# Attention step with scores and keys in alternation, maxima in the middle, batch work last but one

## What is computed

```python
qkv = jnp.einsum('bsh,oh->bso', hidden_states, w_qkv)      # hidden_states: normalized rows
scores = jnp.einsum('bhqd,bhkd->bhqk', q, k) * scale
scores = jnp.where(causal, scores, jnp.finfo(scores.dtype).min)
probs = jax.nn.softmax(scores, axis=-1)
attn = jnp.einsum('bhqk,bhkd->bhqd', probs, v)
return jnp.einsum('bsh,oh->bso', attn, w_o)

x = x + 0.5 * _L0_ffn_ref(_layernorm(x, axis=-1), ...)
x = x + _L0_attn_ref(_layernorm(x, axis=-1), L0_attn_w_qkv, L0_attn_w_o)
x = x + 0.5 * _L0_ffn_ref(_layernorm(x, axis=-1), ...)
```

## Time and profile before

| | us |
|---|---|
| median of 3 runs (857.02 to 858.62) | 858.06 |
| profiled execution, its own time | 857.71 |
| span of the profiled execution | 856.0 |
| mean granted TensorE clock, share of full | 0.966 |

### The profile page before, as it was taken

How to read it: one execution, slowest core, us unless ns; L and a number is a source line. 1 busy time by engine, 2 the same in 40 slices (tenths; PEclk the granted TensorE clock), 3 DMA queues, 4 the chain that set the end, 5 groups by cost and what they waited for, 6 DMA issues and landing times. The chain is left out here.

```text
span 856.0 us, 15881 instructions
## 1 busy us (share of the span) xinstructions
PE 766.5 (90%) x6126; PEld 669.7 (78%) x6126; DVE 445.2 (52%) x848; ACT 370.0 (43%) x611; POOL 310.7 (36%) x363
## 2 busy tenths in 40 slices
PE   5789999999999988878788887866799999999997
PEld 3469999999999975555555554444699999999997
DVE  7755444634553037566666576256554446345530
ACT  4215445534553111555554556423154455345531
POOL 3164454455413361141321122201644544554133
PEclk9999999999999996989999999898999999999999
DMA  9434554254322242221022010052345543543222
GB/s 331 115 98 114 140 139 114 60 150 128 93 55 26 26 160 88 77 77 73 7 77 101 21 59 28 20 179 53 95 111 144 139 111 65 150 127 92 58 25 25
DMA packets 60070, 80.27 MB, mean 94 GB/s; under 512 B 11140, under 2 KB 46980, under 8 KB 59988
## 3 DMA queue, kind: packets, MB, share of 16 engines
q1 hardware_dynamic: 44660, 60.35, 21.0%
q0 software_dynamic: 15360, 19.23, 12.3%
HBM read 51.72 MB, written 19.01 MB: 83 GB/s over the span
## 5 line engine op out<-in xcount | busy, mean ns | idle before, releaser
L610 DVE SCALAR_TENSOR_TENSOR first_h_lo<-first_ps_h,first_h_hi 128x320 fp32r<-128x320 f32 x128 | 62.9, 492 | 104.5 <-ACT first_h_hi L469 104.5
L610 DVE SCALAR_TENSOR_TENSOR second_h_lo<-second_ps_h,second_h_hi 128x320 fp32r<-128x320 f32 x128 | 62.9, 492 | 104.5 <-ACT second_h_hi L469 104.5
L386 POOL DMA_INDIRECT after_first<-first_scaled,first_add_now x40 | 69.4, 1734 | 115.7 <-ACT first_scaled L462 113.2
L386 POOL DMA_INDIRECT out_dram<-second_scaled,second_add_now x40 | 69.2, 1729 | 115.7 <-ACT second_scaled L462 113.2
L1104 DVE TENSOR_REDUCE at_maxima<-at_ps_front 128x4 f32<-128x512 f32 (+2 forms) x96 | 96.3, 1038 | 15.6 <-PE at_ps_front L1232 15.3
L986 POOL TENSOR_SCALAR_AFFINE_SELECT at_probs<-at_probs 128x512 f32<-128x512 f32 x64 | 39.9, 635 | 172.6 <-ACT at_probs L1044 171.7
L1044 ACT ACTIVATE at_probs<-at_ps_keys 128x768 f32<-128x768 f32 (+1 forms) x96 | 81.9, 877 | 25.1 <-PE at_ps_keys L1263 23.0
L721 PE MATMUL first_ps_o<-first_w_hi,first_h_hi 128*128 128x256 f32 x320 | 91.2, 285 | 0.0
L721 PE MATMUL second_ps_o<-second_w_hi,second_h_hi 128*128 128x256 f32 x320 | 91.2, 285 | 0.0
L721 PE MATMUL first_ps_o<-first_w_lo,first_h_hi 128*128 128x256 f32 x320 | 90.0, 281 | 0.0
L721 PE MATMUL second_ps_o<-second_w_lo,second_h_hi 128*128 128x256 f32 x320 | 90.0, 281 | 0.0
(11 more groups left out here) (271 smaller groups left out, 1755.4 us busy)
## 6 DMA issues: line engine op xcount, KB each, us to landing
first_w_raw<-in_L_ffn_w_dram SPq DMA_DIRECT2D x16, 1024.0 KB, 8.5
second_w_raw<-in_L_ffn_w_dram SPq DMA_DIRECT2D x16, 1024.0 KB, 6.7
at_q_stack<-at_pre_hi SPq DMA_DIRECT2D x16, 256.0 KB, 2.4
at_k_stack<-at_pre_hi SPq DMA_DIRECT2D x16, 256.0 KB, 2.5
x<-_attn_hidden_states_dram SPq DMA_DIRECT2D x4, 512.0 KB, 5.7
normed_rows<-first_xn SPq DMA_DIRECT2D x4, 512.0 KB, 6.5
x<-after_first SPq DMA_DIRECT2D x4, 512.0 KB, 6.1
at_q_stack<-at_pre_lo SPq DMA_DIRECT2D x8, 256.0 KB, 2.6
```

The costliest lines, as they stand in the source:

```text
L386: pool.indirect_dma_start(sum_rows, bass.IndirectOffsetOnAxis(ap=add_now[par][:, s:s + 1], axis=0), scaled[par][:, s, :], None, bounds_che ...
L610: v.scalar_tensor_tensor(h_lo[:, f, a * HALF:(a + 1) * HALF], ps_h[:, f % 2, a, 0:HALF], 0.0, h_hi[:, f, a * HALF:(a + 1) * HALF].bitcast( ...
```

## The change

The order that `step_plan` writes is changed, and nothing else. `S[n]` and `N[n]` are the scores and keys groups of the step.

```diff
         if v < -1:
-            return normal + work + sum(S, [])
-        return (normal + S[0] + N[0] + S[1] + N[1] + turns + N[2] + S[2] + N[3] + S[3] + work + outputs + S[4] + N[4] + S[5] +
-                N[5] + project)
+            return work + sum(S, []) + normal
+        return (N[0] + S[0] + S[1] + N[1] + S[2] + N[2] + S[3] + N[3] + normal + turns + N[4] + S[4] + project +
+                outputs + S[5] + work + N[5])
```

## The result

| | us |
|---|---|
| changed kernel, median of 4 runs (836.02 to 837.06) | 836.74 |
| kernel before on the same chip, median of 4 runs (857.02 to 861.36) | 858.34 |
| ratio, 95% interval | 0.9735, 0.9716 to 0.9754 |
| profiled execution after: its own time, its span | 837.06, 835.3 |

The account below looks back on a forecast made before the run. A chain of waits through several engines, set by two score buffers, bounds attention. Periods 19.2, start 3.0 and tail 1.9, less 2.6 for clock falls, give 21.5 us off 857.71: 836.2; forecast 836, range 826 to 849.

Parts of the forecast that it names:

- W behind S5: Batch work moved behind the sixth score group, starting 0.40 us after outputs end: stacks periods 11.94, values 11.76, rows 11.26.
- Rows and heads: Attention periods: rows take 11.26 us; the four head transposes cost TensorE about 0.53 in each of five periods.
- Alternation gains nothing: Reordering score and key groups alone: a plain attention period sums to 9.84 us against 9.80 and 9.78 measured.
- Normalize: Normalize moved behind the fourth key group: its 1.93 us of VectorE costed at nothing, at most 0.5 each.
- T behind N3: Turned maxima behind the fourth key group: fourth score group stops waiting for heads; if outputs fail to cover, 1.0 us each returns.
- P in front of O: Projection moved ahead of outputs: 3.3 us each (3.0 to 3.6), its addition and statistics lying under the outputs.
- Start, tail and falls: Start gains 3.0 us (1 to 4.5), tail 1.9 (0 to 5.3); two clock falls at 1.3 lose 2.6.
- low period: Attention clock rivals: falls in every period, about 848 us, chance 0.15; low clock holds, about 872, chance 0.06.
- wait of T for a maximum: Sign in normalize steps: the turning of maxima on TensorE would wait no more than 1 us for a maximum.
- wait of N0 for a transfer: Rival: the next unit's first key group waits for late transfers of turned maxima; about 843 us, chance 0.08.
- S1's wait for W: Rival: second score group waits for batch work's halves as long as outputs did; 844 us, chance 0.05.
- TensorE's waits for ScalarE's exponentials: Sign of a wrong prediction: TensorE waiting for exponentials in attention periods; ScalarE busy 7.93 us in its fullest period.

Follow-up runs that it names:

- both filled ones: Changed kernel with first normalize back in front and dummy matmuls in start and tail: 832.06 us; the same with more dummy matmuls at the start: 830.20 us.

## Why the prediction was right

**W behind S5.** Right, and the core of the gain: alone in the kernel before it gives 11.16 of the 19.85. The size was off for stacks, 12.43 against 11.94: W starts 0.56 behind O instead of 0.40, and from S1 to O's end it takes 7.31 (401.77 to 409.08) instead of 7.05. Values came to 12.17 (with normalize) and about 12.1 without heads (12.37 less 0.25), against 11.76. Here TensorE itself is nearly full, which the sum did not see: it went by the chain S1 to S4.

**Rows and heads.** 11.29 for both together, against 11.26 and 0.53. Heads cost 0.25 (period 12 less period 13, 10.31 less 10.06), not 0.53; that they fall where TensorE would have waited fits, but is not shown apart.

**Alternation gains nothing.** Half right. A plain period went from 9.80 to 10.06, where 9.84 was forecast; longer plain periods were one of the signs by which the prediction called itself wrong, and they came, by 0.26. The chain is the one that was summed, and the term that grew is the negation: 0.97 from the end of S5's reduction to the start of S0's (500.59 to 501.56) where 0.74 was put, with GpSimd's masks beside it from 500.39 to 501.61. VectorE in period 13 of the changed kernel:

```profile
500.62 0.43 DVE L1113 TENSOR_SCALAR at_minus_max<-at_maxima 128x16 fp32r<-128x16 f32 x1
501.09 0.55 DVE L1114 SCALAR_TENSOR_TENSOR at_minus_max<-at_maxima,at_minus_max 128x16 f32<-128x16 f32 x1
```

But under the other moves the order is worth about 3.6, as the old order put back shows. The step that failed is that it was weighed in a plain period alone, where no W crowds the keys groups.

**Normalize.** The size was right, the reason wrong. It costs nothing now, but not because it stands behind N3: back in front it costs nothing either (12.35), behind N3 without W's move its period is 2.01 longer (a fall among it), and W's move alone hides it (13.81 twice). The timeline of VectorE in period 6 shows it at its new place, ended in time for O's division:

```profile
417.55 1.40 DVE L1074 BATCH_NORM_STATS2 stats<-x 128x6 f32<-128x256 f32 x4
...
419.47 0.68 DVE L1121 TENSOR_TENSOR at_heads_t_lo<-at_ps_front,at_heads_t_hi 128x512 fp32r<-128x512 f32 x1
420.07 1.21 DVE L1104 TENSOR_REDUCE at_maxima<-at_ps_front 128x2 f32<-128x1024 f32 x1
421.58 0.26 DVE L1132 RECIPROCAL at_inverse_sum<-at_ps_keys 128x16 f32<-128x16 f32 x1 [0.30 <-PE at_ps_keys L1282]
```

**T behind N3.** Right: S3 does not wait for heads any more, and with T early again a period with heads costs the 1.0 and more that were named as the price of a missing cover.

**P in front of O.** Right: 2.97 and 2.93 (15.40 and 15.36 less 12.43) against 3.3, a little below the stated 3.0 to 3.6. Its addition and statistics run under O: in period 7 they take VectorE from 434.22 to 437.00, O takes TensorE from 434.02 to 436.85.

**Start, tail and falls.** Three terms missed, and the misses cancel; that the sum came out within 1 us is in part luck. The start gave 2.1 instead of 3.0: the first normalize cost 1.03 instead of 1.93, but the values that leave it and the first two steps with keys, put at 4.9, gave only 3.1. The tail gave 2.6 instead of 1.9, with 1.5 lost behind it. The two falls at 1.3 did not come: none of the twelve periods is below 1.00. That made up for periods longer by 1.42 (147.92 less 146.5). The price of a fall was right (0.56 to 1.86 measured). What the clock gave is not the order's gain, though: four of the twelve periods had fallen before, and dummy matmuls alone won back 3.9 in three of them, so by an estimate from these some 4 of the 17.74 is clock. Periods 3 to 13 stand in the changed order in four traces (changed, first normalize in front, both filled ones), and no fall came there. But the order of a period does not settle it: the kernel with normalize in front lost 1.51 in a period whose own items stand as in the change, and falls of 0.82 to 0.91 came in six of the other seven variants. What decides a single fall stays open.

**The rivals.** None held in the changed kernel: no low period, no wait of T for a maximum, no wait of N0 for a transfer, S1's wait for W 0.44. TensorE's waits for ScalarE's exponentials, a further sign named, stay at 0.2 or less, 0.5 in all twelve periods.

## What to carry to other kernels

With two buffers in rotation, as here, long work belongs right behind the point where its buffer comes free and the other engine starts its run of reductions; which item stands two places ahead of it among the users of those buffers decides whether it starts at once. Price such a reordering as a whole: parts undone one by one lost more than twice what all of them gained, and a cheap step hidden by one move is easily credited to another. Dummy matmuls paid where the clock stayed low for many microseconds (2.90 in the start); for a single fall they won 0.6 to 1.9, and the kernel before as a whole was no faster with them.

## What the runs showed of the hardware

The low clock can hold through busy work: in the changed kernel the windows 328 to 336 and 336 to 344 are both at 0.50, with TensorE busy 5.73 and then 7.24 of 8.00 us; four dummy matmuls per scores group held it at 1.00 over the same work. The first normalize, which moved with them, is not the cause: moved alone it leaves both windows at 0.50.

Small VectorE operations are slower beside GpSimd. In the changed kernel both negations of a unit take 0.17 or 0.18 in the eleven units where GpSimd does nothing beside them; in the other five, one or both take 0.36 to 0.55. In the kernel before, GpSimd works beside them in fourteen of the sixteen units, and one or both take 0.29 to 0.58 there. First VectorE in the changed kernel:

```profile
374.94 0.36 DVE L1113 TENSOR_SCALAR at_minus_max<-at_maxima 128x16 fp32r<-128x16 f32 x1
375.33 0.50 DVE L1114 SCALAR_TENSOR_TENSOR at_minus_max<-at_maxima,at_minus_max 128x16 f32<-128x16 f32 x1
```

GpSimd beside it, in the changed kernel:

```profile
374.16 2.18 POOL L978 TENSOR_SCALAR at_xn<-x,at_inverse,at_offset 128x256 f32<-128x256 f32 x4
```

The same two operations of VectorE in the kernel with normalize back in front:

```profile
371.99 0.18 DVE L1113 TENSOR_SCALAR at_minus_max<-at_maxima 128x16 fp32r<-128x16 f32 x1
372.19 0.18 DVE L1114 SCALAR_TENSOR_TENSOR at_minus_max<-at_maxima,at_minus_max 128x16 f32<-128x16 f32 x1
```

GpSimd works beside both in the first case and is idle in the second (its masks end at 370.71). The Trainium skill (SBUF — State Buffer, "SBUF: two separate sides") says that GpSimd and VectorE share one pair of ports, VectorE when it runs in a mode that uses two ports or reads two inputs from SBUF beside a GpSimd instruction that reads it, and that whichever starts first holds the pair for its whole instruction while the other waits. The rows agree with it: the extra 0.18 and 0.32 are less than one of GpSimd's four instructions (2.18 by 4, 0.55). The second negation reads two inputs; whether the first runs in such a mode, no run here shows. No run set the effect apart by itself. It cost nothing in this period, 12.43 and 12.44, where W covers it; in a plain period the negation is on the path.
